# Attention scores of two heads at once: fp32 products in four row groups in place of float32r products over 128 rows

## The reference

```python
a = _layer_norm(audio_kv, ln_gamma, ln_beta)
Q = (hidden_states @ Wq.T).reshape(B, Tt, HEADS, HEAD_DIM).transpose(0, 2, 1, 3)
K = (a @ Wk.T).reshape(B, Ta, HEADS, HEAD_DIM).transpose(0, 2, 1, 3)
V = (a @ Wv.T).reshape(B, Ta, HEADS, HEAD_DIM).transpose(0, 2, 1, 3)
scores = jnp.einsum('bhtd,bhsd->bhts', Q, K) * scale
scores = jnp.where(mask, scores, jnp.float32(-jnp.inf))
attn = jax.nn.softmax(scores, axis=-1)
out = jnp.einsum('bhts,bhsd->bhtd', attn, V)
return hidden_states + jnp.tanh(gate) * (out @ Wo.T)
```

## Time and profile before

| | us |
|---|---|
| median of 3 executions | 3441.61 (3440.38 to 3449.8) |
| the profiled execution | 3439.03 |
| its span, first to last instruction | 3437.2 |
| PE busy | 3294.5 |
| DVE busy | 2639.9 |
| ACT busy | 1860.6 |

### The profile page before, as it was taken

One profiled execution on the slowest core, in us unless ns is written; L12 is line 12 of the kernel. 1 busy time (PEld: TensorE's weight loads), 2 busy tenths in 40 slices (PEclk: granted clock), 3 DMA queues, 4 the chain that ended last, 5 costly groups with the idle time before them and its releaser, 6 DMA issues.

```text
span 3437.2 us, 74851 instructions
## 1 busy us (share of the span) xinstructions
PE 3294.5 (96%) x31856; PEld 2491.6 (72%) x31856; DVE 2639.9 (77%) x3721; ACT 1860.6 (54%) x3086; POOL 234.2 (7%) x460
## 2 busy tenths in 40 slices
PE   5889999999999999999999999999799899998998
PEld 4667777878777787877777877777566566666666
DVE  3888888888888888888888888886546666566566
ACT  2455555555555555555545555554346656556555
POOL 1000000000000000000000000000011010010110
PEclk9999999999999999999999999999899999999999
DMA  3113323233332232332323233323244224133222
GB/s 111 62 69 111 117 93 120 93 123 111 111 111 103 104 112 101 113 119 106 123 88 119 93 108 112 109 107 120 97 110 97 66 60 115 38 84 104 56 66 53
DMA packets 91914, 336.65 MB, mean 98 GB/s; under 512 B 16704, under 2 KB 37824, under 8 KB 65600
## 3 DMA queue, kind: packets, MB, share of 16 engines
q0 software_dynamic: 39936, 234.91, 20.8%
q1 hardware_dynamic: 51216, 93.68, 8.6%
q10 hardware_dynamic: 432, 3.28, 0.2%
HBM read 252.11 MB, written 16.78 MB: 78 GB/s over the span
## 4 chain that ended last, share of the span: by engine, by line
PE 90%; DVE 6%; ACT 3%; issue 1%; DMA 0%; SPq 0%; ACTq 0%; DVEq 0%
PE psum L718 40%; PE psum L727 5%; PE psum L787 5%; PE psum L888 5%; PE psum L764 5%; PE psum L906 3%; PE psum L858 3%; PE psum L848 3%; PE psum L878 3%; DVE psum L1717 2%; PE psum L863 2%; PE psum L673 2%; PE psum L683 1%; PE psum L623 1%; PE psum L661 1%; PE psum L659 1%
## 5 line engine op out<-in xcount | busy, mean ns | idle before, releaser
L718 PE MATMUL psum<-rw 128*128 128x256 f32 x6144 | 1412.6, 386 | 14.6 <-DVE rw L1515 11.3
L718 PEld LDWEIGHTS psum<-rw 128*128 128x128 f32 x6144 | 1166.5, 193 | 227.2 <-issue 55.4
L1627 DVE TENSOR_TENSOR rw<-rw 128x2048 f32<-128x2048 f32 x192 | 429.5, 2279 | 15.0 <-ACT rw L1201 14.5
L1717 DVE CUSTOM_DVE_ANT_0 psum<-psum,mem 128x1024 f32<-128x1024 f32 x256 | 313.6, 1225 | 83.9 <-PE psum L878 83.7
L1275 ACT ACTIVATE rest<-psum,mem 128x1024 f32<-128x1024 f32 x256 | 285.1, 1114 | 80.1 <-DVE mem L1717 78.4
L888 PE MATMUL psum<-ident,rest 128*128 128x128 f32 x2048 | 269.6, 275 | 0.2 <-ACT mem L1268 0.2
L1142 ACT ACTIVATE rw<-psum 128x512 f32<-128x512 f32 x192 | 111.6, 593 | 290.7 <-PE psum L718 290.5
L1904 POOL DMA_DIRECT2D rw<-big_dram x192 | 101.9, 531 | 2382.3 <-PE psum L718 2369.8
L888 PEld LDWEIGHTS psum<-ident,rest 128*128 128x128 f32 x2048 | 235.2, 141 | 38.5 <-issue 13.1
L1509 DVE SCALAR_TENSOR_TENSOR rw<-psum,rw 128x256 f32<-128x256 f32 x480 | 196.4, 476 | 71.9 <-PE psum L673 52.9
L1080 ACT ACTIVATE rw<-rw 128x256 f32<-128x256 f32 x192 | 99.7, 590 | 271.0 <-DVE rw L1459 271.0
(11 more groups left out here) (150 smaller groups left out, 4515.0 us busy)
## 6 DMA issues: line engine op xcount, KB each, us to landing
rw<-big_dram POOLq DMA_DIRECT2D x192, 1024.0 KB, 5.1
side<-mem POOLq DMA_DIRECT2D x256, 128.0 KB, 4.3
rw<-xs_dram SPq DMA_DIRECT2D x32, 512.0 KB, 3.3
side<-mem SPq DMA_DIRECT2D x256, 64.0 KB, 2.1
rw<-rw SPq DMA_DIRECT2D x192, 64.0 KB, 1.9
xs_dram<-rw SPq DMA_DIRECT2D x24, 512.0 KB, 2.7
rw<-x_dram SPq DMA_DIRECT2D x16, 512.0 KB, 3.3
mem<-xs_dram SPq DMA_DIRECT2D x16, 512.0 KB, 4.5
```

The source lines that it names most:

```text
L718: last = mm(t[:, o * TC:(o + 1) * TC], big[:, k, P * m:P * m + P], src[:, k, 0:TC], start=k == 0, stop=k == KT - 1, skip_group_check=True)
L1627: state_dve.inc(tt(s_bd[:, half, :, :].rearrange("p c (h j) -> p c h j", h=4), own, place, ALU.mult), it, f"b{k}{half}")
L1717: maxima.inc(nc.vector.tensor_tensor_reduce(t, t, mbias.rearrange("p (a s) -> p a s", a=2), 1.0, 3.4e38, ALU.add, ALU.min, accum_out=mx[:, ...
```

## The change

A step of PE is now a turn of two heads. The four heads of a group lie in the 32-row quarters of the key and query tiles as their products leave them (`k_own`, `q_own`), as plain fp32. A second pair of tiles (`k_side`, `q_side`) holds the same with the two halves of the partitions exchanged, made by four transfers on SP per group; POOL copies nothing any more. `scores` opens both places of `s_ring`, and issues four products of 32 rows by 512 columns: two heads times two halves of the keys, each in its own row group and its own bank. All four channel tiles of keys and queries have places of their own (four instead of two), the values two instead of one and a part. The second part on DVE is gone. BESIDE is rewritten for 32 turns per batch, with the tiles packed into the first part of a batch; the load of the next context is moved ahead of the stores.

```diff
-Q_PART, K_PART = (0, 0, 1, 1), (0, 1, 0, 1)
-LAG = 3
+TURNS = HEADS // 2
+PER_BATCH = TURNS // B
...
+BESIDE = {0: [(0, "v5")], 1: [(0, "v6")], 2: [(0, "v7")], 3: [(0, "k10")], 4: [(0, "k11")], 5: [(0, "q1")], 6: [(0, "k20")], 7: [(0, "k21")],
+          8: [(0, "k30")], 9: [(0, "k31")], 10: [(-1, "wo0")], 11: [(-1, "wo1")], 12: [(-1, "wo2")], 13: [(-1, "wo3")], 14: [(0, "q2")], 15: [(1, "mean0")],
+          16: [(1, "mean1")], 18: [(0, "q3")], 19: [(1, "var")], 20: [(1, "q0")], 21: [(1, "rstd0"), (1, "rstd1")], 23: [(1, "k00")], 24: [(1, "k01")],
+          26: [(1, "v0")], 27: [(1, "v1")], 28: [(1, "v2")], 30: [(1, "v3")], 31: [(1, "v4")]}
...
+def turned_in(m):
+
+    return [[n] if 0 <= n < HEADS else [] for n in (2 * m - 3, 2 * m - 2)]
+
+
+def summed_in(m):
+
+    return [(m - 3) // 2] if m % 2 == 1 and m >= 3 else []
...
             def side_by_side(group):
...
-                for g in range(HPT):
-                    for h in range(HPT):
-                        to, of = slice(AD * g, AD * g + AD), slice(AD * h, AD * h + AD)
-                        sp.dma_start(q_side[group % 2][to, h, :], q_part[of, Q_PART[g], :]).then_inc(q_laid[group % 2], 16)
+                sp.dma_start(q_side[low, n, :], q_own[high, n, :]).then_inc(laid[n], 16)
+                sp.dma_start(q_side[high, n, :], q_own[low, n, :]).then_inc(laid[n], 16)
+                sp.wait_ge(*d_ring.empty_at(b, f"k{e}1"))
+                sp.dma_start(k_side[low, n, :], k_own[high, n, 0:512]).then_inc(laid[n], 16)
+                sp.dma_start(k_side[high, n, :], k_own[low, n, 512:SK]).then_inc(laid[n], 16)
...
             def scores(n):
...
-                t = opened(s_ring, n, "s")
+                two = [opened(s_ring, n + i, "s") for i in range(2)]
+                last = [None, None]
                 for sh in range(2):
-                    last = mm(t[:, sh, :], q_side[group % 2][:, h, P * q:P * q + P].bitcast(F32R), k_side[group % 2][:, h, sh * 512:sh * 512 + 512].bitcast(F32R),
-                              start=True, stop=True)
-                s_ring.fill(last, n, "s")
+                    for i in range(2):
+                        rows = slice(2 * AD * sh + AD * i, 2 * AD * sh + AD * i + AD)
+                        if h == 2 * sh:
+                            queries, keys = q_own, k_own[rows, group % KT, 512 * sh:512 * sh + 512]
+                        else:
+                            queries, keys = q_side, k_side[rows, group % KT, :]
+                        last[i] = mm(two[i][:, sh, :], queries[rows, group % KT, P * q:P * q + P], keys, start=True, stop=True)
+                for i in range(2):
+                    s_ring.fill(last[i], n + i, "s")
...
-            for n in range(HEADS + LAG + 1):
-                if n < HEADS:
-                    scores(n)
-                if n % HPT == HPT - 1 and n >= HPT:
-                    weighted(n // HPT - 1)
-                if 0 <= n - LAG < HEADS:
-                    turned(n - LAG)
-                for b, name in beside(n):
+            for m in range(TURNS + 2):
+                first, second = turned_in(m)
+                if m < TURNS:
+                    scores(2 * m)
+                for n in first:
+                    turned(n)
+                for b, name in beside(m):
                     batch_tile(b, name)
+                for block_ in summed_in(m):
+                    weighted(block_)
+                for n in second:
+                    turned(n)
...
-            def second_part(b, name):
...
+                if m < TURNS:
+                    maximum(2 * m)
+                for n in first:
+                    turned(n)
+                if m < TURNS:
+                    maximum(2 * m + 1)
+                for b, name in beside(m):
+                    after(b, name)
+                for block_ in summed_in(m):
+                    block_out(block_)
+                for n in second:
+                    turned(n)
```

More of the change, by code:

```diff
@@ L99, in other_tiles @@
         tiles += of(0, name)
-    for n in range(HEADS + LAG + 1):
-        tiles += [(n // HPT - 1, "out", "dve")] if n % HPT == HPT - 1 and n >= HPT else []
-        tiles += [(n - LAG, "t", "dve")] if 0 <= n - LAG < HEADS else []
-        for b, name in beside(n):
+    for m in range(TURNS + 2):
+        first, second = turned_in(m)
+        tiles += [(n, "t", "dve") for n in first]
+        for b, name in beside(m):
             tiles += of(b, name)
+        tiles += [(k, "out", "dve") for k in summed_in(m)]
+        tiles += [(n, "t", "dve") for n in second]
     return tiles + [(B - 1, f"wo{m}", "dve") for m in range(KT)]
@@ L266, in build @@
         gate = sb("gate", [P, 2])
[L267 to L271 removed]
+        rw = sb("rw", [P, RW_COLS])
         def part_of(name, pattern=None, **dims):
@@ L279, in view @@
             at, size = AT_AT[name]
-            after = at - SIDE_AT - SIDE_COLS
-            v = rest[:, after:after + size] if after >= 0 else mem[:, at:at + size]
+            v = rw[:, at:at + size]
             return v.rearrange(pattern, **dims) if pattern else v
@@ L413, in build @@
         gate_ready = sem("gate_ready")
[L414 removed]
+        laid = [sem(f"laid{n}") for n in range(KT)]
         d_ring = Ring(psum, (0, 1), sem("d_ring_full"), {"act": sem("d_ring_act"), "dve": sem("d_ring_dve")}, other_tiles())
@@ L1414, in _ @@
                     stream(n, "g", 1)
-            for n in range(HEADS + LAG + 1):
-                for b, name in beside(n - 1):
-                    after(b, name)
-                if n % HPT == HPT - 1 and n >= HPT:
-                    inverse_sums(n // HPT - 1)
-                if 0 <= n - LAG < HEADS:
-                    turned(n - LAG)
-                if n < HEADS:
-                    exponentials(n)
-                for b, name in beside(n - 1):
+            for m in range(TURNS + 2):
+                first, second = turned_in(m)
+                for n in first:
+                    turned(n)
+                if m < TURNS:
+                    exponentials(2 * m)
+                    exponentials(2 * m + 1)
+                for b, name in beside(m):
+                    after(b, name)
+                for block_ in summed_in(m):
+                    inverse_sums(block_)
+                for n in second:
+                    turned(n)
+                for b, name in beside(m):
                     if name[:4] == "mean":
@@ L1428, in _ @@
                 for sh in range(2):
-                    for b, name in beside(n - 1 - sh):
+                    for b, name in beside(m - sh):
                         if name == f"rstd{sh}":
```

142 lines of the change are left out of this document (54 added, 88 removed), and 3 rows, old and new, of the table BESIDE.

## The result

The changed kernel takes 3481.4 us (median; 3477.3 to 3484.3), beside 3442.1 for the kernel before on the same chip: a ratio of 1.0109, interval 1.0093 to 1.0125. It is slower, which was held the likeliest of the three, but the time lies above the range of 3434 to 3474. The profiled execution is 3482.07, its span 3480.0 against 3437.2: +42.8.

A forecast was written before the change was run, and what follows sets the result against it. PE bounds places with batch tiles, the scores-maximum-exponential chain those without. Batch 0 +0.7, batches 1 and 2 -4.3 together, batch 3 +13.1 and its end +1.5 make +11.0 on the 3441.6 median: 3453 us, range 3434 to 3474 (8 in 10).

The forecast's parts named there:

- the likeliest of the three: Chances for the whole kernel's time: slower 0.48, within 0.3% (3431 to 3452) 0.38, faster 0.14.
- Turns with a tile: Attention-stage turns of two heads holding a full batch tile, PE-bound: 6.40 us even, 8.54 us odd.
- rival (b): Scores on PE: row groups overlap less than in L673; a quarter of the bounds' gap gives +27, 3480 us; chance 0.12.
- Rival (c): Scores on PE: entry into the tiling is hidden, up to -33 us, at half that 3436; chance 0.18.
- the products save PE nothing: Scores and following transposes on PE: 1.07 + 0.15 us against 0.94 before, per turn of two heads.
- rival (a): Even turns without a tile: PE standstill lowers the granted clock, some 1 us each in batch 3, +14, 3467; chance 0.15.
- the tail: End of batch 3, from turn 30 to the output products: 17.5 us against 16.1 before, +1.5 with rounding.
- The 91 turns with PE as the bound: Turns where a hidden tiling entry would save PE time, up to -33 us in total.
- The odd turn without a tile: Turn with the weighted sum but no batch tile, where that sum waits for DVE's copy: 5.88 us.
- The variance turn 19: Turn of batches 0 to 2 preparing the next batch, with a tile of 1.9 in four column groups: 7.1 us.
- The even turn without a tile: Turn bound by the chain of scores, maximum, copy, second maximum, exponential: 5.50 us, PE needing 2.96.
- at nothing: Second parts on DVE (12 per batch), fewer copies per group and POOL's 256 issues, all priced at no time.

The follow-up runs named there:

- the float32r experiment: Changed kernel with scores again as float32r products over 128 rows, order, places and transfers kept, values not the real scores: 3447.4 us, ratio 1.0009.

## Why the prediction was off

**Right: the prices at full clock.** Turns with a tile came to 6.40 and 8.55 (6.40 and 8.54), and batches 1 and 2 would be within 2.1 us of their forecast at the full clock. The pair of scores goes from start to next line in 1.07 and prints 1.14, exactly as L673 does with three row groups; the fourth group found room, and rival (b) is excluded. The Trainium skill, "TensorE: Matmul & The Clock Gate", section "Measured speedup vs the span model", has 3.07 times for four row tiles; the prediction's estimate from it, 1.12, lies 0.05 above the trace, and the measurement decides. Rival (c), a hidden entry, is excluded by the same rows. The statement that the products save PE nothing and cost 0.28 per turn was right to 0.01 in the turns that PE bounds, by the float32r experiment.

**Wrong: the clock, which the sum left out as rival (a).** It was priced at some 1 us per turn on 14 turns of batch 3, chance 0.15, on the ground that PE busy 2.54 of 5 us had lost the clock and 2.93 of 5 had not the earlier trace rows. It happened: 15.7 us in the turns of the table above, of which 8.4 in batch 3 (17, 23, 25, 27 and 29: 1.5 + 1.5 + 2.65 + 1.5 + 1.25), 4.1 in batch 0 and 1.6 each in batches 1 and 2. Some 1.3 of the tail's 18.9 are the same (the weighted sum at 3453 prints 2.32 instead of 1.96). Three things in the step failed. The price of a fall is 1.1 to 2.7, because the lower level lasts through the transposes and the weighted sum, not through the pair of scores alone. It also strikes outside batch 3, behind turns 10 and 12 of batch 0 and turn 22 of batches 0 to 2, which I never looked at for this. And it fell in 10 turns of 128, not behind all thin ones, as a price of 1 us on every such turn had it. That the rival's +14 comes near the 17.0 of turns and tail together is luck: fewer falls, dearer ones, and half of them in other batches. The two rows lay on either side of the turn in question, one with a lowered clock and one without. With nothing to choose between them, a chance of 0.15 was far too small, and the range should have held the case together with dearer turns. The upper end does not follow from its own text either: half of (b)'s 27 on 3453 is 3467, not 3474. (The 91 turns with PE as the bound are 87 by the table; that changes little.)

**Wrong: the smaller terms, +9.5 together.** Three are seen in rows.

- The odd turn without a tile, 6.07 for 5.88. The chain of waits of turn 21 in batch 3 (L1734 the copy, L917 the weighted sum):

```profile
3385.35 1.21 DVE psum L1729
...
3386.62 0.56 DVE rw L1734
3387.18 0.14 issue
3387.32 1.95 PE psum L917 x64
3389.27 1.02 PE psum L900 x8
```

  From the weighted sum to the next scores it is 2.90, since the transposes behind it cost 1.02. I had taken 2.73 from a stretch of before, where the float32r scores print 0.84 behind the start of those transposes, though I had named the 1.02 myself.

- The variance turn 19, 8.40 for 7.1: the sum missed ScalarE's square root. Timeline of PE and ACT in batch 1:

```profile
2910.29 1.28 ACT L1255 ACT_TABLE_LOAD   x1
2911.58 0.47 ACT L1255 ACTIVATE rw<-psum,eps 128x256 f32<-128x256 f32 x1
...
2912.20 1.06 PE L900 MATMUL psum<-ident,rw 128*128 128x128 f32 x8 [1.22 <-ACT rw L1255]
```

  A table load of 1.28 and the root of 0.47 stand ahead of the freeing of the place that PE's transposes want: 1.22 of standstill. A second load of 1.28, back to the exponential, stands in turn 20 (2915.57), also missing from the sum.

- The even turn without a tile, 5.61 for 5.50: from the second exponential to the next scores 1.35 (3407.67 to 3409.02), not 1.25 as in the earlier trace rows; the chain of waits has 1.21 for the exponential and 0.14 for the "issue" behind it, where I had taken 0.04 for a hand-over the earlier trace rows. Turns 17 (+0.57), 20 (-0.14) and 22 (-0.36), turn 0 of batches 1 to 3 (6.58 for 6.40) and the shares of the tail are what is left.

**Wrong, but without effect on the sum: "at nothing".** I wrote that the second parts stood in none of the waits of the earlier trace rows. They did not stand in those rows, but the earlier trace rows is a stretch without a batch tile, and the earlier trace rows were read for PE's own prices only; the wait of 0.55 in front of the next tile lies 4 us ahead of them. The second part cost the kernel before 18 us, measured in the old order. The forecast did not suffer, since the turns of after were priced from their parts and the sum compared with measured batches. But the text missed the one gain in the change, and with it that the rest of the change costs 55: 21.5 for the order of turns and 34.0 for the products.

**The account.** Forecast +11.0; clock in turns 15.7; clock in the tail 1.3; turn prices and rest 9.5 (the difference that is left, and what the periods at the full clock add up to); together 37.5, the measured growth of the stage. The copies of keys and queries were not late, as worked out: the turns ahead of a new group (7, 15 and 23, apart from the clock) and the first ones of it have their usual length; turn 0 of batches 1 to 3 is 0.18 longer, but comes back to 6.40 when DVE does both maxima first, with the same transfers.

**Open.** Which thin turns lower the clock is not settled. Within one execution turn 20 of batch 3 leaves turn 21 at the full clock, and turn 24, the same work (PE busy 3.04 of 5.61 in both), leaves turn 25 at 0.61. Falls move to other turns when some are removed, once into turn 17, whose own standstill had not mattered before, and a shorter standstill in a shorter turn made them worse. What is shown is that the falls of the changed kernel go when the thin turns ahead of them are filled, and that batch 3 with a tile in every even turn but 28 and 30 had none until the one behind turn 30. What part of the order's 21.5 would be left at the full clock, by my estimate from the turns about 8, was not tried.

## To carry to other kernels

When two short steps are joined into one longer hold of the same buffers, the work that hid each of them is lost: price the new chain, and count the stretches of low TensorE activity that it makes as a term of the sum, at the lower clock and over everything that follows them. An operation that waits for another engine in front of a critical one on an in-order queue can cost more than its own length (0.82 for 0.69 in block 2 here) or nothing (the blocks with one tile); 45 of them, 31 us of DVE's time, cost 18: look for it in the turns where the bound engine seems full, not only where it stands still, and move it to an engine with nothing to do. Splitting precision into two rounded operands over all 128 rows cost less TensorE time here than plain fp32 in four row groups.

## What the hardware showed

- Four row groups run side by side: eight fp32 records of 0.43, 3.44 one behind the other, take 1.07 from start to the next line, which is two rounds and 0.21 more. The transposes behind them take 1.02 for 0.87, as behind the column groups.
- The granted clock fell behind a single turn of 5.61 us with PE busy 3.04 (turn 10 of batch 0, then 0.77), and not behind every such turn; a turn of 6.07 became one of up to 8.72.
- POOL's subtraction of 128x512 in SBUF takes 1.29, DVE's with one side in PSUM 0.69.
- Nearly the same code ahead of the stage ended at 2532.1 to 2542.5 in eleven traces, a spread of 10 us that I cannot tie to the edits.
